# Products that nothing reads, put ahead of seven waits of TensorE in a decoder layer

## The reference

```
x = x + attn_ref(layernorm(x), W_q, W_k, W_v, W_o)            # 16 heads of 16, rotary, causal softmax
x = x + xattn_ref(layernorm(x), ctx, ctx, mask, ...)          # 16 heads of 64, 77 context rows
x = x + ffn_ref(layernorm(x), W_fc, b_fc, A_fc, B_fc, ...)    # 256 -> 1024 -> 256, 8-bit fake quantised
                                                              # weights plus a rank-16 LoRA part, gelu
```

## Time and profile before

| what | us |
|---|---|
| median of 3 runs | 640.81 |
| lowest and highest of them | 640.13, 643.83 |
| the profiled execution, its device time | 644.52 |
| its span, first to last instruction | 642.8 |
| TensorE busy in the span | 531.2 (83%) |
| mean granted TensorE clock | 0.937 |

### The profile page before, as it was taken

One profiled execution on the slowest core, in us unless ns is written; L12 is line 12 of the kernel. 1 busy time (PEld: TensorE's weight loads), 2 busy tenths in 40 slices (PEclk: granted clock), 3 DMA queues, 4 the chain that ended last, 5 costly groups with the idle time before them and its releaser, 6 DMA issues.

```text
span 642.8 us, 11809 instructions
## 1 busy us (share of the span) xinstructions
PE 531.2 (83%) x4334; PEld 451.6 (70%) x4334; DVE 392.6 (61%) x1093; ACT 301.7 (47%) x484; POOL 250.1 (39%) x317
## 2 busy tenths in 40 slices
PE   2388779778987989889979997999899799958955
PEld 2376657656666777878778776878887687847755
DVE  4757531867858943796489539946963683554332
ACT  2333364331544745166445654672755167426323
POOL 5820022644453363155262517262454006522210
PEclk9689999976988979899999999999999799988969
DMA  5589999943210523042224222226140501111000
GB/s 187 168 237 184 189 206 238 283 131 128 71 51 1 160 55 88 8 152 64 75 75 121 71 71 87 75 59 119 51 112 3 155 22 41 37 41 37 1 16 17
DMA packets 63709, 62.45 MB, mean 97 GB/s; under 512 B 6868, under 2 KB 60804, under 8 KB 63652
## 3 DMA queue, kind: packets, MB, share of 16 engines
q1 hardware_dynamic: 62148, 56.74, 33.9%
q0 software_dynamic: 1504, 4.95, 2.2%
HBM read 38.28 MB, written 23.10 MB: 95 GB/s over the span
## 4 chain that ended last, share of the span: by engine, by line
PE 52%; DVE 19%; ACT 9%; DMA 7%; issue 5%; POOL 4%; SPq 3%; DVEq 0%; ACTq 0%; POOLq 0%
PE banks L797 8%; PE banks L798 7%; PE banks L799 7%; PE banks L955 5%; DVE banks L2379 4%; PE banks L1057 4%; PE banks L1046 4%; PE banks L932 4%; PE banks L1119 3%; DMA k_stack<-rot_dram 3%; DMA fold_raw<-fold_dram 2%; PE banks L969 2%; ACT probs L1749 2%; DMA fold_dram<-work 2%; PE banks L831 1%
## 5 line engine op out<-in xcount | busy, mean ns | idle before, releaser
L2379 DVE CUSTOM_DVE_ANT_0 banks<-banks,causal_qk 128x256 f32<-128x256 f32 (+1 forms) x256 | 84.0, 385 | 19.5 <-PE banks L932 17.8
L564 POOL TENSOR_TENSOR work<-work,rc 128x616 f32<-128x616 f32 x32 | 40.5, 1265 | 103.1 <-DVE rc L2479 103.1
L581 POOL TENSOR_SCALAR_AFFINE_SELECT probs<-probs 128x256 f32<-128x256 f32 x128 | 53.2, 442 | 65.4 <-ACT probs L1749 65.3
L571 POOL TENSOR_TENSOR fold_lo<-fold_raw,fold_hi 128x616 fp32r<-128x616 f32 x32 | 48.7, 1524 | 47.5 <-ACT fold_hi L1717 47.5
L1717 ACT ACTIVATE work<-banks 77x512 f32<-77x512 f32 (+1 forms) x72 | 43.2, 601 | 48.9 <-PE banks L1046 45.4
L1749 ACT ACTIVATE probs<-banks 128x768 f32<-128x768 f32 x64 | 51.8, 809 | 29.8 <-PE banks L955 29.3
L932 PE MATMUL banks<-k_stack,q_stack 96*128 96x256 f32 (+1 forms) x256 | 42.9, 293 | 19.9 <-DVE mneg L2379 9.2
L2477 DVE TENSOR_REDUCE sm<-work 128x8 f32<-128x616 f32 x32 | 25.4, 793 | 50.8 <-ACT work L1779 50.7
L932 PEld LDWEIGHTS banks<-k_stack,q_stack 96*128 96x128 f32 x256 | 37.1, 202 | 26.6 <-DVE mneg L2379 11.3
L2334 DVE TENSOR_TENSOR late<-banks,late 128x512 fp32r<-128x512 f32 x40 | 27.4, 685 | 38.0 <-ACT late L1717 38.0
L955 PE MATMUL banks<-q_stack,k_stack 100*128 100x128 f32 (+1 forms) x256 | 46.1, 303 | 5.1 <-ACT probs L1749 2.3
(11 more groups left out here) (190 smaller groups left out, 1569.5 us busy)
## 6 DMA issues: line engine op xcount, KB each, us to landing
fold_raw<-fold_dram SPq DMA_DIRECT2D x32, 308.0 KB, 3.0
fold_dram<-work SPq DMA_DIRECT2D x8, 616.0 KB, 8.3
rot_dram<-rot_s_hi SPq DMA_DIRECT2D x16, 256.0 KB, 2.8
rot_dram<-rot_s_lo SPq DMA_DIRECT2D x16, 256.0 KB, 3.4
q_stack<-rot_dram SPq DMA_DIRECT2D x32, 128.0 KB, 2.7
k_stack<-rot_dram SPq DMA_DIRECT2D x32, 128.0 KB, 3.0
fold_dram<-fold_raw SPq DMA_DIRECT2D x4, 616.0 KB, 6.1
fold_dram<-fold_raw_hi SPq DMA_DIRECT2D x4, 616.0 KB, 9.0
```

The costliest lines, as they stand in the source:

```text
L571: pool.tensor_tensor(fold[1][:, :, g % 2], raw[:, :, g % 2], fold[0][:, :, g % 2].bitcast(F32), ALU.subtract).then_inc(g_lo, 1)
L581: last = pool.affine_select(out=diagonal, in_=diagonal, compare_op=ALU.is_ge, fill=0.0, base=0, pattern=[[0, 2], [1, P]], channel_multipli ...
L2379: last = dve.tensor_tensor_reduce(out=held[:, at], in0=held[:, at], in1=bias, scale=-1.0, scalar=HUGE, op0=ALU.add, op1=ALU.min, accum_out ...
```

## The change

TensorE gets a function `fill(at, count)`: count matmuls of a 128x128 piece of the query/key/value weights by a 128x256 piece of the same weights, each into the first half of bank `at`, each starting its own sum. They wait for nothing and signal nothing, and nothing reads what they write. It is called in seven places of the hand-written list, with 24, 24, 14, 28, 8, 4 and 4 matmuls (106 in all). No call of the kernel before is moved or taken away.

```diff
--- before.py
+++ after.py
@@ -1075,6 +1075,10 @@
                                      skip_group_check=True)
                 mm.then_inc(o2_ps, 1)
 
+            def fill(at, count):
+                for _ in range(count):
+                    pe.matmul(halves(at)[:, 0, :], wqkv[0][:, 0, 0:P], wqkv[0][:, 0, 0:W], start=True, stop=True)
+
             def transpose_f(f):
                 pe.wait_ge(xn_f_ok, f + 1)
                 if f == 0:
@@ -1233,6 +1237,7 @@
             transpose_b(0)
             project(2, 1)
             scores2(0, 0)
+            fill(6, 24)
             scores(1, 0, 3)
             scores(1, 1, 3)
             scores2(0, 1)
@@ -1639,12 +1644,14 @@
             weigh2(6, 3)
             output_a(7)
             output2(6, 3)
+            fill(2, 24)
             transpose_b(7)
             transpose_f(6)
             scores2(7, 0)
             narrow(6)
             hidden(6, 0)
             hidden(6, 1)
+            fill(2, 14)
             hidden(6, 2)
             hidden(6, 3)
             scores2(7, 1)
@@ -1670,12 +1677,16 @@
             weigh2(7, 3)
             project_down(6, 3)
             output2(7, 3)
+            fill(2, 28)
             transpose_f(7)
+            fill(2, 8)
             narrow(7)
+            fill(2, 4)
             hidden(7, 0)
             hidden(7, 1)
             hidden(7, 2)
             hidden(7, 3)
+            fill(2, 4)
             project_down(7, 0)
             project_down(7, 1)
             project_down(7, 2)
```

## The result

Over 20 runs of each kernel the median went from 641.1 to 637.85 us (the changed kernel 633.61 to 642.66). The ratio is 0.9955, 95% interval 0.9935 to 0.9975: 0.45% faster, 2.9 us, where 0.98% and 6.3 us were forecast. The time lies in the stated range (631.0 to 639.0), but the gain is a little under half of the forecast. The profiled execution has a span of 640.2 us, 2.6 less than before.

What follows compares the result with a forecast made beforehand. TensorE, busy 83% of the span, was taken to pay twice: it waits, then works at half clock. Gains of 1.6 + 1.3 + 0.4 + 3.0 = 6.3 us take the median from 640.81 to 634.5; range 631.0 to 639.0.

Steps and rivals of the forecast that it cites:

- All seven end before their wait does: cost nothing: All seven fills, 106 products at 0.12 us each: each ends within TensorE's wait, so they add no time.
- the first place: Fill of 24 ahead of element 1's first scores: full clock behind it gains 1.6 us, ends 0 and 3.0.
- The last block: `transpose_f(7)` to `hidden(7, 1)`, a chain with nothing beside it: 3.0 us gained, ends 1.0 and 3.1.
- The middle: Fills ahead of `transpose_b(7)` and `hidden(6, 2)`: gains of 1.3 and 0.4 us.
- Taken: 1.3: At `transpose_b(7)` and `transpose_f(6)`: `scores2(7, 0)` at full rate brings `narrow(6)` 1.3 us earlier, and that passes on.
- 0 if the clock falls anyway: Lower end of the gain at `transpose_b(7)` and `transpose_f(6)`, whose upper end was 1.5 us.
- The 0.4 for `hidden(6, 2)`: Fill of 14 ahead of `hidden(6, 2)`: full clock gains 0.4 us, as gelu also waits for `hid_lo`.
- upper end of 1.16: Most that full clock at `hidden(6, 2)` could gain: the 1.16 us ScalarE's third gelu was idle for it.
- 24 products take 2.9 us in a wait of 3.6: First fill, ahead of element 1's first scores: it fits inside the wait for the keys' DMA, costing nothing.
- (b): Rival: clock falls anyway in one place, or the lead at element 1's scores is absorbed; 636 to 637.5 us, chance 0.25.
- (d): Rival: fills run late, at half clock or 0.21 us per product; 4.7 us late, 645.5 us, chance 0.05.
- (a): Rival: all half-rate busy time comes back, 9.5 us and more; 631 down to 629 us, chance 0.10.

## Why the prediction was right or wrong

**The reading of the chip held.** Half-rate stretches stand behind TensorE's waits; products that nothing reads keep the clock; each costs 0.12 us at full rate; fills within their wait delay nothing. The earlier trace rows priced these well: 28 took 3.51 against 3.4 foretold. "All seven end before their wait does: cost nothing" didn't hold at the first place (below).

**The last block: 3.0 foretold, about 2.4 measured.** Of seven profiles without a fill there the last stretch has a mean of 18.79 us (18.32 to 19.31), six with all four have 16.34 to 16.36. The profile that I worked from was near the long end with 19.16; against it the difference is 2.8. `hidden(7, 0)` came 0.94 earlier after the transposes instead of 1.0. A right mechanism, its term a fifth too large on average, and most of that is the one long profile.

**The middle: 1.3 + 0.4 foretold, nothing in the changed kernel's profile, about 1 on average.** This is the second step that failed, "Taken: 1.3". With 24 products the clock held in two of three profiles (16.62, 16.79) and fell in one (18.22); ten without a fill have 17.48 to 19.61, mean 18.58. The two that held had 1.08 of idle time behind the fill, the one that fell 1.43; three profiles make no rule of that. What the end "0 if the clock falls anyway" described happens in a part of the executions, and my working made it a rival with a chance of its own instead of a factor on the term. Of the gain, 0.4 goes again: from the first `transpose2` of element 7 to `transpose_f(7)` it takes 32.67 to 32.77 in three of the four kernels where the clock held in the middle, 32.26 to 32.32 elsewhere. The 0.4 for `hidden(6, 2)` fits the profile that I worked from (6.06 to 5.72 is 0.34), but only because the fall there was a short one: it is 1.4 to 1.5 where the clock stays low for 6.8 us, and nothing where it holds anyway, 0.8 on average over the ten profiles without the 14. My upper end of 1.16 was too low.

**The first place: 1.6 foretold, none measured.** This is the step that failed most, and it is the sentence "24 products take 2.9 us in a wait of 3.6": the cost was put at nothing. 3.6 was one execution's wait, and I had looked only at the keys, not at the rotation on VectorE that the scores wait for as well. In ten profiles without that fill the scores started 5.04 to 8.53 us after `transpose_b(0)`, and the fill ends at 6.94, so it costs up to 1.9 us, 0.7 on average. It cost the full 1.9 in the changed kernel's own profile. What it gives behind has to be compared like with like. In the five early profiles the stretch behind is 53.38 on average without it, in the two early ones with it 51.75 (51.16, 52.34): 1.6, the term as forecast. But the fill cost 1.5 there (6.94 against 5.49), and 0.2 is left. In the late ones it costs nothing, and one profile (53.89 against 54.42) gives 0.5. So the gain behind was right in size in the early executions and was eaten by the cost. These are few profiles, and the ratios neither prove nor exclude what is left; the kernel with 12, in which nearly all of the cost is gone, should have gained more than its 0.9997. That part stays open.

**The sum.** 2.4 + 1.0 + 0.2 to 0.5 is 3.6 to 3.9, beside the measured 2.9 (1.6 to 4.2 by the interval). The shortfall against 6.3 is the first fill, then the middle, then the last block.

**The rivals.** (b), one place lost, came true, twice over: the clock fell behind `transpose_b(7)`, and the first place's lead was gone before `transpose_b(7)`. It was priced at 636 to 637.5 for one such loss; there were two, and 637.85 was measured. That its price fits is in part luck: it has the first place's 1.6 lost later, and in the early executions it went to the fill itself. (d) didn't come, but a fill past its wait did, and 1.9 was paid where (d) named 1.5; I had looked for lateness from slow products, not from a short wait. (a) is refuted by the last stretch, where 6.6 us of busy half-rate time gave 2.4 to 2.8. What the Trainium skill says of short idles (TensorE: Matmul & The Clock Gate, A second HAM failure mode: psum-queue depth-cycling) was a better guide at `transpose_b(7)` than my 1.3 taken whole: 1.43 us idle and thin work behind the fill were enough in one of three profiles, and the kernel in which the idle was closed held the clock in its profile.

## What to carry to other kernels

Products that nothing reads are worth placing where TensorE waits for a chain of other engines of fixed length, and the work behind that wait is TensorE's own on the path that sets the end; the sparse stretch behind the wait needs its fills as well, or more than half of the gain is lost (2.4 us in the last block with them, 0.9 with the large fill alone). Ahead of a wait for a DMA, take the length of the fill from the shortest wait in several profiles, not from one, and look at every semaphore of the wait: what reaches past it delays the work behind by its full length. And where a lead arises far from the end of a long run, expect other falls of the clock to scatter the time by more than the lead.

## What I had not expected of the hardware

Two profiles of one and the same kernel, from different sessions, differ by 8.1 us in span (642.8 and 634.7); on one chip 35 executions of it went from 634.7 to 643.05. The wait ahead of the first scores of element 1 is 0.8 to 4.3 us long from profile to profile, in two groups, and ahead of it the DMA engines had been busy without a break (265 GB/s from 110 to 124 us in the kernel before). The chip may be part of it: all four profiles of one session have the keys early, all three of another late, the others both. The wait for element 7 is steadier, at 3.2 to 4.4. Falls of the clock at 227 to 265 and near 385 us come in some executions and not in others, without a change of the code there: the changed kernel's profile has both, and needs 384.58 us for a run that takes 377.2 to 378.6 in eleven of the other fourteen.
